# A fused two-layer transformer block: the value products on both halves of the weight columns, in one piece per unit

## Chip, cores and metric

One core of a Trainium2 chip (TensorE = PE for matmuls, VectorE = DVE, ScalarE = ACT, GpSimd = POOL, SyncE = SP, which issues the DMAs). The metric is the device time of one execution in microseconds (us), the median of three runs.

## What is computed

Two transformer layers over x of 1024 tokens by 256 (float32). The change is in the first layer's attention, 16 heads of a latent-attention kind. Cut to what matters:

```python
q = (rmsnorm(h @ q_a_w.T) @ q_b_w.T)          # per head 128 columns without, 64 with rotary embedding
kv = rmsnorm(kv_lora) @ kv_b_w.T              # kv_lora: 1024 keys x 64, shared by the heads
q_pe, k_pe = apply_rope(q_pe, ...), apply_rope(k_pe, ...)
probs = softmax(concat(q_nope, q_pe) @ concat(k_nope, k_pe).T * 192 ** -0.5)
main_out = (probs @ v) @ o_w.T                # v: 128 columns per head
x = x + ga * (gates[0] * main_out + gates[1] * pattern_out)
```

The kernel folds the key and value weights into its query and output weights, so that the keys are 64 latent plus 64 rotary rows per head, and the values are the same 64 latent columns for all heads (`kvx`).

## The kernel before

Engines run lists of steps written by hand (`main_order()` makes the one that matters, MAIN) and meet only by semaphores. MAIN treats 32 **units**: unit u is head pair u // 4 and 256 of the 1024 queries. A unit has four score tiles i = 0 to 3 (head i % 2, 128 queries), each 128 queries by 1024 keys.

For a tile, PE makes the scores (`pe_score`, six matmuls of 512 columns, L1805 to L1807, into one of two double banks; slot i % 2 is free once the exponential two tiles earlier has read it), DVE takes the maximum (`dve_score`, L1814), ACT the exponential with its sum (`act_expo`, L1829), and DVE turns the probabilities in blocks of 32 by 32 (`dve_turn`, L1842) into `PT`: 32 blocks b of 32 keys, each with 128 columns (2 heads x 2 x 32 queries), where the partitions 32g to 32g+31 hold the queries of group g (g = 0 to 3).

The value products of unit u-1 (`pe_pvm`, L1908) are done in **loop** u of `main_order()`, beside the scores of unit u: for each b and g one float32 matmul with 32 rows, 64 weight columns (the values `kv4`) and 128 moving columns, summed over b in PSUM bank 4+g, partitions 0 to 63. The profile shows two records for each float32 matmul, so 256 a unit. Loop u, in the order of the steps:

- step 0: scores (u, 0); projection of unit u-2 (`pe_project_out`, L1935) and its addition to x on DVE (`dve_add_out`, L1948); reciprocals of unit u-1's sums (`dve_recip`, L1862 to L1869); the turn of tile (u-1, 3); exponential (u, 0)
- step 1: scores (u, 1); turn (u, 0); exponential (u, 1)
- step 2: scores (u, 2); value products of u-1, blocks 0 to 15; turn (u, 1); exponential (u, 2)
- step 3: scores (u, 3); blocks 16 to 31; `act_lift` (L1916: the second head's 64 columns from partitions 0 to 63 to 64 to 127); `dve_weigh` (L1926: times the reciprocals `Rs`, into `OTm`); exponential (u, 3); turn (u, 2)

SP sends each unit's reciprocals out (`sp_shares`, L1877, four DMAs after `dve_recip`) and back spread over 64 partitions (`sp_spread`, L1890, two DMAs), in time for `dve_weigh`. The sums, the scores' second bank pair and all other products share PSUM banks 4 to 7, so PE's value products wait for the last `dve_weigh`, and for the copies of all products issued before them (`COPIED`).

Beside this, the tiles of the next head pair p are prepared by six **products** (`PREP_AT` says at which tile numbers, counted from 16(p-1); `FIRST` in what order): four rotary ones R0 to R3 (keys twice, queries twice) and two latent ones Q0, Q1. Each is five or six matmuls of 512 columns on PE (`pe_prep`, L1566); a copy on ACT to the one buffer `t12` (`act_product`, L1600), which waits until the product before has left it; for a rotary product four DMAs on SP that swap rows (`sp_swap`, L1610, after POOL's sum of the rotary product before); and POOL's work (`pool_product`, L1622 to L1648: cosine, sine, sum, rounding, remainder). Scores of a new head pair wait for POOL's parts. Two products that share a loop are called a pair below.

Of the kernel before, what the change touches and what calls it, by code (L numbers as in the profile page):

```python
# [8 lines left out]
F32 = mybir.dt.float32  # L9
# [3 lines left out]
ALU = mybir.AluOpType  # L13
ACT = mybir.ActivationFunctionType
# [57 lines left out]
    (31, 1): [("normed", 0)],  # L72
}

PREP_AT = ((4, 5, 8, 9, 12, 13), (0, 1, 4, 8, 9, 12))


def main_order():

    order = [("expo", 0, 1), ("score", 0, 2), ("ctx", 0), ("ctx", 1), ("vturn", 0, 0), ("expo", 0, 2), ("score", 0, 3),  # L80
             ("cadd", 0), ("ctx", 2), ("vturn", 0, 1), ("cadd", 1), ("expo", 0, 3), ("ctx", 3), ("cadd", 2), ("vturn", 0, 2),
             ("cadd", 3)]
    preps = {16 * (p - 1) + at: (p, i) for p in range(1, 8) for i, at in enumerate(PREP_AT[p > 1])}

    def prep(n):
        if n in preps:
            order.extend([("prep", *preps[n]), ("pcopy", *preps[n])])

    def output(u):
        if u >= 0:  # L90
            order.extend([("project", u), ("add", u)])

    for u in range(1, 32):
        order.append(("score", u, 0))
        output(u - 2)
        prep(4 * u)
        order.extend([("rec", u - 1), ("vturn", u - 1, 3), ("expo", u, 0)])
        order.extend(BESIDE_LAST.get((u, 0), ()))
        order.append(("score", u, 1))
        prep(4 * u + 1)  # L100
        order.extend([("spread", u - 1), ("vturn", u, 0), ("expo", u, 1)])
        order.extend(BESIDE_LAST.get((u, 1), ()))
        order.extend([("score", u, 2), ("pv", u - 1, 0), ("vturn", u, 1), ("expo", u, 2)])
        order.extend([("score", u, 3), ("pv", u - 1, 1), ("lift", u - 1), ("ot", u - 1), ("expo", u, 3), ("vturn", u, 2)])
    output(30)
    order.extend([("rec", 31), ("vturn", 31, 3), ("turn", 0), ("spread", 31), ("pv", 31, 0), ("pv", 31, 1), ("hT", 0),
                  ("wup", 1), ("wdown", 1), ("lift", 31), ("ot", 31), ("project", 31), ("logits", 0), ("add", 31)])
    return order
# [191 lines left out]

R0, R1, R2, R3, Q0, Q1 = ("rope", 0), ("rope", 1), ("rope", 2), ("rope", 3), ("lat", 0), ("lat", 1)

FIRST = (R0, R1, R2, Q0, Q1, R3)


def program(nc, a, out):
    def sem(name):
        return nc.alloc_semaphore(name)
# [6 lines left out]
    def sb(name, shape, dt, at=None):  # L315
        if at is None:
            at = base[0]
            base[0] += size_of(shape, dt)
        return nc.alloc_sbuf_tensor_at(name, list(shape), dt, offset=at)
# [14 lines left out]
    rest = nc.alloc_psum_tensor("bank4", [128, 4, 512], F32)  # L334
# [40 lines left out]
    WSP = A.at  # L375
# [90 lines left out]
    PTl = [sb(f"PTl{i}", [128, 16, 128], F32, at=at) for i, at in enumerate((KV, WKPE))]  # L466
    kv4 = [sb(f"kv4{i}", [128, NT, 64], F32, at=at) for i, at in enumerate((W0A, HN, MP.at, S0 + 88 * 1024))]
    OTm = sb("OTm", [128, 256], F32, at=LNW)
    Rs = sb("Rs", [128, 2, 256], F32, at=vx_end)
    wks = sb("wks", [128, 2, 128], F32, at=vx_end + 2048)  # L470
    wkl = sb("wkl", [128, 2, 128], F32R, at=vx_end + 2048)
# [105 lines left out]
    silu_ok = sem("silu_ok")  # L577
# [1177 lines left out]
    op_tr, op_cT, op_mm, op_add, op_g, op_x = (sem(n) for n in ("op_tr", "op_cT", "op_mm", "op_add", "op_g", "op_x"))  # L1755

    d_kv, pt_ok, lift_ok = sem("d_kv"), sem("pt_ok"), sem("lift_ok")
    d_shares, d_spread = sem("d_shares"), sem("d_spread")
    for s_ in MAIN:
        if s_[0] == "score":  # L1760
# [21 lines left out]
    def transposed(u, b):  # L1782
        return PTl[b // 16][:, b % 16, :] if u == 31 else PT[u % 2][:, b, :]
# [109 lines left out]
    def pe_pvm(e, u, part):  # L1893

        if part == 0:
            if u:
                e.wait_ge(ot_ok[1], u)
                e.wait_ge(add_ok, u)
            else:
                e.wait_ge(op_cT, 4)  # L1900
                e.wait_ge(cadd_ok, 4)
                e.wait_ge(d_kv, 256)
            e.wait_ge(*COPIED[u])
            e.wait_ge(pt_ok, 4 * u + 4)
        for b in range(16 * part, 16 * part + 16):
            for g in range(4):
                rows = slice(32 * g, 32 * g + 32)
                last = e.matmul(rest[0:64, g, 0:128], kv4[b % 4][rows, b // 4, :], transposed(u, b)[rows, :],  # L1908
                                start=(b == 0), stop=(b == 31), skip_group_check=True)
        if part:  # L1910
            last.then_inc(pv_mm[1], 1)

    def act_lift(e, u):

        e.wait_ge(pv_mm[1], u + 1)
        e.activation(rest[64:128, :, 0:64], rest[0:64, :, 64:128], ACT.Copy).then_inc(lift_ok, 1)  # L1916

    def dve_weigh(e, u):

        e.wait_ge(pv_mm[1], u + 1)  # L1920
        e.wait_ge(lift_ok, u + 1)
        e.wait_ge(d_spread, 32 * (u + 1))
        if u:
            e.wait_ge(pr_mm, u)
        by_row = "p (j g q) -> p j g q"
        e.tensor_tensor(OTm[:].rearrange(by_row, j=2, g=4), rest[:, :, 0:64].rearrange("p g (j q) -> p j g q", j=2),  # L1926
                        Rs[:, u % 2, :].rearrange(by_row, j=2, g=4), ALU.mult).then_inc(ot_ok[1], 1)

    def pe_project_out(e, u):

# [1328 lines left out]
```

## Time and profile before

| | |
|---|---|
| runs | 1345.41, 1345.27, 1342.64 us; median 1345.27 |
| profiled execution | 1341.48 us, span of its trace 1339.7 us |
| MAIN's loops | from some 275 us to 805 us of the span |
| busy, share of the span | PE 94%, DVE 65%, ACT 47%, POOL 40% |
| granted PE clock | 0.992 of full speed on average |
| DMA | 66 MB, 49 GB/s on average |

"Busy" of PE counts from a matmul's start to its end; matmuls overlap, so starts tell more than durations. In a timeline row, the first number is the start in us, the second the time covered; the number behind "x" counts the merged instructions. In square brackets stands how long the engine had been idle before it, and what released it.

### The profile page before, as it was taken

Reading aid. Unit: us, or ns where it says so; the run is one execution under the profiler, and the core shown is the slowest. Engines: PE = TensorE matmul, PEld = TensorE weight load, DVE = VectorE, ACT = ScalarE, POOL = GpSimd, SP = SyncE. Lnnn points to the kernel's source line nnn. Section 1 sums busy time; section 2 is a strip of 40 time slices with the busy share of each in tenths; the row PEclk is TensorE's granted clock in tenths of the full one; section 3 lists DMA queues with packets and bytes.
Section 4 is the critical chain, followed back from the end, with each engine's and each line's share of the span. In section 5 each row is a group of like instructions: output and inputs, shape, how many; then the busy total and the mean of one; then the engine's idle time right before and its main releaser. Section 6 shows DMA issues by size and latency. Waiting matters only on the chain. (4 is left out here: it accounts for less than half of the span.)

```text
span 1339.7 us, 34528 instructions
## 1 busy us (share of the span) xinstructions
PE 1260.0 (94%) x14433; PEld 920.9 (69%) x14436; DVE 868.1 (65%) x1322; ACT 634.1 (47%) x1210; POOL 531.6 (40%) x531
## 2 busy tenths in 40 slices
PE   8999999998999999999999998999998998899998
PEld 5544443487777777777777777788864344678997
DVE  4789888165666666666666775645677764565555
ACT  4489888733333333333333333433244766435553
POOL 5266363457757474746574203445200000321221
PEclk9999999999999999999999999999999999899999
DMA  7780010020101010101010204011151510101110
GB/s 283 186 173 2 2 28 7 13 53 24 42 18 43 18 42 18 42 18 39 18 38 18 62 11 139 1 47 48 28 121 41 118 37 1 33 13 36 48 40 32
DMA packets 41700, 66.25 MB, mean 49 GB/s; under 512 B 8477, under 2 KB 27677, under 8 KB 40605
## 3 DMA queue, kind: packets, MB, share of 16 engines
q1 hardware_dynamic: 41544, 64.04, 17.6%
q8 instruction: 115, 1.88, 0.6%
q14 instruction: 41, 0.33, 0.1%
HBM read 45.60 MB, written 8.45 MB: 40 GB/s over the span
## 5 line engine op out<-in xcount | busy, mean ns | idle before, releaser
L1908 PE MATMUL bank<-PT,kv 32*64 32x128 f32 x7936 | 231.2, 269 | 24.1 <-ACT t L1600 23.6
L1908 PEld LDWEIGHTS bank<-PT,kv 32*64 32x64 f32 x7936 | 216.4, 132 | 47.2 <-issue 47.2
L1814 DVE TENSOR_REDUCE nmq<-bank 128x1 f32<-128x1024 f32 x128 | 153.4, 1198 | 88.9 <-PE bank L1807 88.8
L1453 ACT ACTIVATE Pb<-bank 128x512 f32<-128x512 f32 (+3 forms) x355 | 180.6, 573 | 30.1 <-PE bank L1432 9.3
L1303 DVE TENSOR_REDUCE mp<-bank 128x2 f32<-128x1024 f32 x128 | 153.5, 1221 | 27.9 <-PE bank L1295 27.0
L1829 ACT ACTIVATE P<-bank,nmq 128x1024 f32<-128x1024 f32 x128 | 141.8, 1110 | 57.9 <-DVE nmq L1814 57.9
L1842 DVE STREAM_TRANSPOSE PT<-P 128x1024 f32<-128x1024 f32 x124 | 151.8, 1224 | 16.9 <-ACT P L1829 16.8
L1805 PE MATMUL bank<-qk1h,qk0h 128*128 128x512 f32 x256 | 109.9, 429 | 7.8 <-ACT P L1829 7.8
L1374 DVE TENSOR_REDUCE mpc<-bank 128x2 f32<-128x1024 f32 (+2 forms) x96 | 88.3, 953 | 43.2 <-PE bank L1362 22.1
L1475 PE MATMUL bank<-Pb,vx 128*17 128x256 f32 (+3 forms) x1222 | 105.1, 403 | 0.7 <-ACT OTa L1489 0.5
L1807 PE MATMUL bank<-qk1h,qk0l 128*128 128x512 f32 x256 | 101.0, 395 | 0.0
L1806 PE MATMUL bank<-qk1l,qk0h 128*128 128x512 f32 x256 | 100.6, 393 | 0.0
L1916 ACT ACTIVATE bank<-bank 64x256 f32<-64x256 f32 x32 | 11.4, 357 | 187.9 <-PE bank L1908 187.9
L1600 ACT ACTIVATE t<-bank 128x512 f32<-128x512 f32 x48 | 28.7, 598 | 113.4 <-PE bank L1566 68.1
L1622 POOL TENSOR_TENSOR Rt<-t,cosT 128x512 f32<-128x512 f32 x32 | 41.0, 1282 | 104.1 <-ACT t L1600 102.3
L2086 POOL TENSOR_TENSOR cTt<-cTt,gab 128x256 f32<-128x256 f32 x8 | 6.1, 759 | 182.0 <-DVE cTt L2081 181.9
L2312 POOL TENSOR_TENSOR hl<-hf,hh 128x512 fp32r<-128x512 f32 x32 | 41.8, 1306 | 87.1 <-ACT hh L2299 87.1
L1926 DVE TENSOR_TENSOR OTm<-bank,Rs 128x256 f32<-128x256 f32 x32 | 13.6, 424 | 91.2 <-ACT bank L1916 91.2
L1432 PE MATMUL bank<-qstr,kstr 64*128 64x512 f32 x256 | 70.9, 494 | 0.6 <-ACT Pb L1453 0.6
L1805 PEld LDWEIGHTS bank<-qk1h,qk0h 128*128 128x128 f32 x256 | 47.9, 187 | 33.5 <-ACT P L1829 15.1
L2526 POOL TENSOR_TENSOR v1l<-wr,v1h 128x512 fp32r<-128x512 f32 x25 | 32.1, 1286 | 95.3 <-ACT v1h L2521 95.3
L1432 PEld LDWEIGHTS bank<-qstr,kstr 64*128 64x128 f32 x256 | 28.2, 183 | 56.8 <-ACT Pb L1453 36.1
(353 smaller groups left out, 2921.9 us busy)
## 6 DMA issues: line engine op xcount, KB each, us to landing
t<-t SPq DMA_DIRECT2D x128, 64.0 KB, 2.0
wr<-wf SPq DMA_DIRECT2D x25, 256.0 KB, 2.7
wraw<-wf SPq DMA_DIRECT2D x8, 768.0 KB, 4.5
scratch<-stgr SPq DMA_DIRECT2D x4, 1024.0 KB, 4.0
Rs<-shares SPq DMA_DIRECT2D x64, 64.0 KB, 2.7
scratch<-stg SPq DMA_DIRECT2D x8, 384.0 KB, 2.6
qst<-scratch SPq DMA_DIRECT2D x9, 256.0 KB, 8.1
owT<-owT SPq DMA_DIRECT2D x1, 2048.0 KB, 11.4
```

Of the source, the lines that this page charges most:

```text
L1303: e.tensor_reduce(mp[:, w % 3, :, j, kh], wide[slot][:], AX, ALU.max).then_inc(ring_ok, 1)
L1374: e.tensor_reduce(mpc[:, w // 2 % 3, a0:a0 + 2, j, kh], wide[slot][:, :, 0:c], AX, ALU.max).then_inc(ring_ok, 1)
L1432: e.matmul(bank[b][:], kst2[r, hp, kt * 128:kt * 128 + 128], qst2[r, hp, cols(half)], start=True, stop=True).then_inc(st_mm[0], 1)
L1453: e.activation(PBR[l][i % len(PBR[l])][:, 0:c], bank[b][:, 0:c], ACT.Exp, scale=0.25).then_inc(exp_ok[0], 1)
L1475: last = e.matmul(bank[6][32 * a:32 * a + 17, to:to + c], vx[:, t, h * 17:h * 17 + 17], PBR[l][i % len(PBR[l])][:, q0:q0 + c], start=(t == ...
L1805: e.matmul(o, qh[:, qs], kh[:, ks], start=True, stop=False)
L1806: e.matmul(o, qh[:, qs], kl[:, ks], start=False, stop=False)
L1807: last = e.matmul(o, ql[:, qs], kh[:, ks], start=False, stop=True)
L1814: e.tensor_reduce(nmq[:, n % 8:n % 8 + 1], scores(u, i), AX, ALU.max, negate=True).then_inc(mp_ok, 1)
L1829: e.activation(probabilities(u, i)[:], scores(u, i), ACT.Exp, bias=nmq[:, n % 8:n % 8 + 1], accum_out=sums[:, u % 2, i:i + 1]).then_inc(ex ...
L1842: e.transpose(PT[u % 2][:, :, c:c + 32], source).then_inc(pt_ok, 1)
L1908: last = e.matmul(rest[0:64, g, 0:128], kv4[b % 4][rows, b // 4, :], transposed(u, b)[rows, :], start=(b == 0), stop=(b == 31), skip_group ...
```

## The change

- `pe_pvm`: blocks b with even number use weight columns 0 to 63 and write partitions 0 to 63 (columns 64 to 191 of each bank); odd ones use weight columns 64 to 127 and write partitions 64 to 127 (columns 0 to 127). Number and size of the matmuls stay.
- each head's sum now lies in two parts. `act_lift` makes two ACT instructions (64 x 256 each) that bring the half that lies on the wrong partitions to an SBUF buffer `other`; `dve_weigh` adds the two (L1934 of the changed kernel) and then multiplies by `Rs` (L1938), which waits for the spread DMAs only there.
- both halves of a unit's value products stand together before the scores (u, 3): one piece of 256 records.
- `PREP_AT` is one row for all head pairs, (5, 8, 9, 12, 16, 17); `FIRST` has R3 before Q1. ACT's copy of a product stands behind the exponential of its step, and SP takes the list `prep` steps as before.

```diff
-PREP_AT = ((4, 5, 8, 9, 12, 13), (0, 1, 4, 8, 9, 12))
+PREP_AT = (5, 8, 9, 12, 16, 17)
...
-    def prep(n):
+    def prep(n, kind):
         if n in preps:
-            order.extend([("prep", *preps[n]), ("pcopy", *preps[n])])
+            order.append((kind, *preps[n]))
...
         output(u - 2)
-        prep(4 * u)
+        prep(4 * u, "prep")
         order.extend([("rec", u - 1), ("vturn", u - 1, 3), ("expo", u, 0)])
+        prep(4 * u, "pcopy")
         order.extend(BESIDE_LAST.get((u, 0), ()))
         order.append(("score", u, 1))
-        prep(4 * u + 1)
+        prep(4 * u + 1, "prep")
         order.extend([("spread", u - 1), ("vturn", u, 0), ("expo", u, 1)])
+        prep(4 * u + 1, "pcopy")
         order.extend(BESIDE_LAST.get((u, 1), ()))
-        order.extend([("score", u, 2), ("pv", u - 1, 0), ("vturn", u, 1), ("expo", u, 2)])
-        order.extend([("score", u, 3), ("pv", u - 1, 1), ("lift", u - 1), ("ot", u - 1), ("expo", u, 3), ("vturn", u, 2)])
+        order.extend([("score", u, 2), ("pv", u - 1, 0), ("pv", u - 1, 1), ("vturn", u, 1), ("expo", u, 2)])
+        order.extend([("score", u, 3), ("lift", u - 1), ("ot", u - 1), ("expo", u, 3), ("vturn", u, 2)])
...
-FIRST = (R0, R1, R2, Q0, Q1, R3)
+FIRST = (R0, R1, R2, Q0, R3, Q1)
...
-                last = e.matmul(rest[0:64, g, 0:128], kv4[b % 4][rows, b // 4, :], transposed(u, b)[rows, :],
-                                start=(b == 0), stop=(b == 31), skip_group_check=True)
+                c = b % 2
+                last = e.matmul(rest[64 * c:64 * c + 64, g, 64 - 64 * c:192 - 64 * c], kv4[b % 4][rows, b // 4, :],
+                                transposed(u, b)[rows, :], start=(b < 2), stop=(b >= 30), skip_group_check=True)
...
-        e.activation(rest[64:128, :, 0:64], rest[0:64, :, 64:128], ACT.Copy).then_inc(lift_ok, 1)
+        if u:
+            e.wait_ge(sum_ok, SUM0 + u)
+        for hd in range(2):
+            e.activation(other[64 * hd:64 * hd + 64, :, :], rest[64 - 64 * hd:128 - 64 * hd, :, 128 * hd:128 * hd + 64],
+                         ACT.Copy).then_inc(lift_ok, 1)
...
-        by_row = "p (j g q) -> p j g q"
-        e.tensor_tensor(OTm[:].rearrange(by_row, j=2, g=4), rest[:, :, 0:64].rearrange("p g (j q) -> p j g q", j=2),
-                        Rs[:, u % 2, :].rearrange(by_row, j=2, g=4), ALU.mult).then_inc(ot_ok[1], 1)
+        by_row = OTm[:].rearrange("p (j g q) -> p j g q", j=2, g=4)
+        e.tensor_tensor(by_row, rest[:, :, 64:128].rearrange("p g (j q) -> p j g q", j=2),
+                        other[:].rearrange("p g (j q) -> p j g q", j=2), ALU.add).then_inc(sum_ok, 1)
+        e.wait_ge(sum_ok, SUM0 + u + 1)
+        e.wait_ge(d_spread, 32 * (u + 1))
+        e.tensor_tensor(OTm[:], OTm[:], Rs[:, u % 2, :], ALU.mult).then_inc(ot_ok[1], 1)
```

How the order moves, at three places. DVE, from the maximum of tile (u, 3) to the turn of (u, 3), before and after:

```order
L1814 TENSOR_REDUCE nmq<-bank 128x1
L1926 TENSOR_TENSOR OTm<-bank,Rs 128x256
L1842 STREAM_TRANSPOSE PT_159<-P_156 128x32x32
L1814 TENSOR_REDUCE nmq<-bank 128x1
L1948 TENSOR_TENSOR x<-x,bank 128x512
```

```order
L1818 TENSOR_REDUCE nmq<-bank 128x1
L1934 TENSOR_TENSOR OTm<-bank,other 128x256
L1938 TENSOR_TENSOR OTm<-OTm,Rs 128x256
L1846 STREAM_TRANSPOSE PT_159<-P_156 128x32x32
L1818 TENSOR_REDUCE nmq<-bank 128x1
L1959 TENSOR_TENSOR x<-x,bank 128x512
```

The first row's maximum reads scores that PE made between the two pieces before, and makes behind the single piece now; the weighing has become two instructions.

ACT in a loop with a pair of products (`P` are exponentials, `t_152` copies of products), before and after:

```order
L1600 ACTIVATE t_152<-bank 128x512
L1829 ACTIVATE P_156,sums<-bank,nmq 128x1024
L1600 ACTIVATE t_152<-bank 128x512
L1829 ACTIVATE P_157,sums<-bank,nmq 128x1024
L1829 ACTIVATE P_155,sums<-bank,nmq 128x1024
L1916 ACTIVATE bank<-bank 64x4x64
```

```order
L1833 ACTIVATE P_156,sums<-bank,nmq 128x1024
L1603 ACTIVATE t_152<-bank 128x512
L1833 ACTIVATE P_157,sums<-bank,nmq 128x1024
L1603 ACTIVATE t_152<-bank 128x512
L1833 ACTIVATE P_155,sums<-bank,nmq 128x1024
L1924 ACTIVATE other<-bank 64x256 x2
```

Each copy has moved behind the exponential of its step.

SP in the loop of R1 and R2 after the change (`t` are the swaps, `shares` and `Rs` the reciprocals out and back):

```order
L1613 DMA t_152<-t_152 32x512 x4
L1881 DMA shares<-rrow 4x32 x4
L1613 DMA t_152<-t_152 32x512 x4
L1699 DMA wks<-wkpe 128x256
L1894 DMA Rs<-shares 64x2x128 x2
```

Before, the loop with R0 and R1 has the same form (with `wqs` ahead of the shares):

```order
L1610 DMA t_152<-t_152 32x512 x4
L1702 DMA wqs<-wqpe 128x256
L1877 DMA shares<-rrow 4x32 x4
L1610 DMA t_152<-t_152 32x512 x4
L1890 DMA Rs<-shares 64x2x128 x2
```

The second swap and the weights' load stand ahead of the spread in both pairs; what has moved is when the second copy lets that swap go.

## Rows read from the trace of the kernel before

**Rows 1.** The page, part 1: busy time of each engine.

```profile
PE 1260.0 (94%) x14433; PEld 920.9 (69%) x14436; DVE 868.1 (65%) x1322; ACT 634.1 (47%) x1210; POOL 531.6 (40%) x531
```

**Rows 2.** Windows: a pair, a pair, one product, none; length, busy (count), clock, DMA share.

```profile
533.22:551.63 18.41, 16.99 (x297) 14.36 (x296) 10.93 (x13) 5.95 (x11) 10.68 (x12) 1.00 0.15 38
...
567.55:585.93 18.38, 16.61 (x295) 14.08 (x294) 10.70 (x13) 5.95 (x11) 11.50 (x13) 1.00 0.06 18
585.93:601.86 15.93, 15.54 (x291) 12.94 (x290) 10.60 (x13) 5.58 (x10) 4.96 (x5) 1.00 0.09 23
768.99:784.03 15.04, 14.40 (x286) 11.99 (x285) 10.61 (x14) 5.19 (x11) 0.00 (x0) 1.00 0.04 10
```

**Rows 3.** Timeline of PE in loop 29, which has no product.

```profile
772.64 0.50 PE L1805 MATMUL bank<-qk1h,qk0h 128*128 128x512 f32 x1
...
777.20 0.50 PE L1805 MATMUL bank<-qk1h,qk0h 128*128 128x512 f32 x1 [0.64 <-ACT P L1829]
...
778.79 3.72 PE L1908 MATMUL bank<-PT,kv 32*64 32x128 f32 x128
782.45 0.50 PE L1805 MATMUL bank<-qk1h,qk0h 128*128 128x512 f32 x1
...
784.03 3.72 PE L1908 MATMUL bank<-PT,kv 32*64 32x128 f32 x128
```

**Rows 4.** Timeline of PE and weight loads with four column tiles, and of both kinds counted.

```profile
204.82 0.63 PE L1475 MATMUL bank<-Pb,vx 128*17 128x256 f32 x8
...
204.80:205.00 0.20, 0.18 (x4) 0.13 (x8) 1.00 0.00 0
...
285.43:285.55 0.12, 0.10 (x4) 0.12 (x8) 1.00 0.00 0
```

**Rows 5.** Timeline of DVE in the same loop 29.

```profile
773.22 0.42 DVE L1926 TENSOR_TENSOR OTm<-bank,Rs 128x256 f32<-128x256 f32 x1 [2.90 <-ACT bank L1916]
773.56 1.23 DVE L1842 STREAM_TRANSPOSE PT<-P 128x1024 f32<-128x1024 f32 x1
774.72 1.19 DVE L1814 TENSOR_REDUCE nmq<-bank 128x1 f32<-128x1024 f32 x1
775.83 0.67 DVE L1948 TENSOR_TENSOR x<-x,bank 128x512 f32<-128x512 f32 x1
...
776.95 1.20 DVE L1842 STREAM_TRANSPOSE PT<-P 128x1024 f32<-128x1024 f32 x1
...
784.14 1.23 DVE L1814 TENSOR_REDUCE nmq<-bank 128x1 f32<-128x1024 f32 x1 [1.47 <-PE bank L1807]
```

**Rows 6.** Timeline of ACT: exponential of loop 29; two copies of a pair.

```profile
775.94 1.12 ACT L1829 ACTIVATE P<-bank,nmq 128x1024 f32<-128x1024 f32 x1 [1.70 <-DVE nmq L1814]
...
609.49 0.60 ACT L1600 ACTIVATE t<-bank 128x512 f32<-128x512 f32 x1 [2.37 <-PE bank L1566]
...
614.11 0.60 ACT L1600 ACTIVATE t<-bank 128x512 f32<-128x512 f32 x1 [2.93 <-DMA t<-t]
```

**Rows 7.** Timeline of PE: value products behind the pair's second copy.

```profile
614.96 3.72 PE L1908 MATMUL bank<-PT,kv 32*64 32x128 f32 x128 [1.34 <-ACT t L1600]
```

**Rows 8.** Timeline of SP's issues, and DMAs by line (last number: us to landing).

```profile
610.12 2.49 SPq L1610 DMA_DIRECT2D t<-t  x4
...
562.13 0.58 SPq L1696 DMA_DIRECT2D wks<-wkpe  x1
...
599.70 1.35 SPq L1890 DMA_DIRECT2D Rs<-shares  x2
...
Rs<-shares SPq DMA_DIRECT2D x64, 64.0 KB, 2.7
```

**Rows 9.** Timeline of POOL: rounding, behind the sum, of the product copied at 609.49.

```profile
616.82 1.28 POOL L1641 CAST qk1h<-Rt 64x512 fp32r<-64x512 f32 x2
```

**Rows 10.** Timeline of PE: value products of the last unit and its projection.

```profile
808.09 7.76 PE L1908 MATMUL bank<-PTl,kv 32*64 32x128 f32 x256 [1.71 <-DVE PTl L1845]
816.81 1.13 PE L1935 MATMUL bank<-mo,OTm 128*128 128x256 f32 x4 [0.96 <-DVE OTm L1926]
```

More of the change, by code:

```diff
@@ L82, in main_order @@
              ("cadd", 3)]
-    preps = {16 * (p - 1) + at: (p, i) for p in range(1, 8) for i, at in enumerate(PREP_AT[p > 1])}
-    def prep(n):
+    preps = {16 * (p - 1) + at: (p, i) for p in range(1, 8) for i, at in enumerate(PREP_AT)}
+    def prep(n, kind):
         if n in preps:
-            order.extend([("prep", *preps[n]), ("pcopy", *preps[n])])
+            order.append((kind, *preps[n]))
     def output(u):
@@ L468, in program @@
     OTm = sb("OTm", [128, 256], F32, at=LNW)
+    other = sb("other", [128, 4, 64], F32, at=WSP + 6144)
     Rs = sb("Rs", [128, 2, 256], F32, at=vx_end)
@@ L1757, in program @@
     d_kv, pt_ok, lift_ok = sem("d_kv"), sem("pt_ok"), sem("lift_ok")
+    sum_ok, SUM0 = silu_ok, 2
     d_shares, d_spread = sem("d_shares"), sem("d_spread")
@@ L1915, in act_lift @@
         e.wait_ge(pv_mm[1], u + 1)
-        e.activation(rest[64:128, :, 0:64], rest[0:64, :, 64:128], ACT.Copy).then_inc(lift_ok, 1)
+        if u:
[3 more added lines that the diff above has]
+                         ACT.Copy).then_inc(lift_ok, 1)
     def dve_weigh(e, u):
         e.wait_ge(pv_mm[1], u + 1)
-        e.wait_ge(lift_ok, u + 1)
-        e.wait_ge(d_spread, 32 * (u + 1))
+        e.wait_ge(lift_ok, 2 * u + 2)
         if u:
             e.wait_ge(pr_mm, u)
-        by_row = "p (j g q) -> p j g q"
-        e.tensor_tensor(OTm[:].rearrange(by_row, j=2, g=4), rest[:, :, 0:64].rearrange("p g (j q) -> p j g q", j=2),
-                        Rs[:, u % 2, :].rearrange(by_row, j=2, g=4), ALU.mult).then_inc(ot_ok[1], 1)
+        by_row = OTm[:].rearrange("p (j g q) -> p j g q", j=2, g=4)
[4 more added lines that the diff above has]
+        e.tensor_tensor(OTm[:], OTm[:], Rs[:, u % 2, :], ALU.mult).then_inc(ot_ok[1], 1)
     def pe_project_out(e, u):
```

## The prediction

> **What bounds the kernel now.** I read the page's busy times first. PE stands at 94% of the span, DVE at 65% [rows 1]. Then the windows of single loops: a loop with a pair of products takes 18.4 us, with one 15.93, with none 15.04, and PE is busy for 14.4 of those 15.04 us, DVE for 10.6 [rows 2]. Loops 2 to 30 are 14 of the first kind, 12 of the second and 3 of the third: 14 x 18.4 + 12 x 15.93 + 3 x 15.04 = 493.9 us. The PE timeline of a loop without product shows where it goes: two pieces of value products take 3.66 and 3.65 us from their start to the next score [rows 3], nearly half the loop. One PE wait is left, 0.64 us before the scores of step 2, for the exponential that frees their bank [rows 3]. In a pair PE waits 1.34 us for the second copy [rows 7]. So PE bounds MAIN, but the chains behind DVE and ACT are close.
>
> **The value products.** Each half piece is 128 records in 3.65 us: four a wave, one for each group of 32 rows, 0.114 us a wave. A wave uses 64 of the 128 weight columns. Do two column halves run beside each other? The trace has a near relative: L1475 has four matmuls with 17 weight columns on four column places. In the first 0.20 us all four first records have started, and all eight records (256 columns, float32) are covered by 0.63 us [rows 4]; one after the other, eight records of twice the columns of a value product could not be done in that time, as each alone would need about a wave of the value products times two, 0.22 us, 1.8 us in all. So column places do overlap, with different moving data. Ends of the range: full overlap, 32 waves of eight, 3.65 us for the 256 records; none, about 7.14 us. I take 3.65, since rows 4 show overlap by four and this asks for two. What could spoil it is the load of weights, eight of 64 columns per 0.114 us; a stretch of eight loads takes 0.12 to 0.13 us in both kinds [rows 4].
>
> A rule speaks against the change. The same rows show eight weight loads in the first 0.12 us of a piece beside only four matmuls, so four loads went to row groups whose matmuls were running [rows 4]. The Trainium skill, TensorE: Matmul & The Clock Gate, Part 3, "The mechanism", says that a weight load overlaps running matmuls only when the row group differs. By that rule nothing would be won from the second column half, and the time would be that of the third rival below; this trace disagrees with it already.
>
> The join of the pieces saves a switch from full array to row groups and back: 784.03 - 782.45 = 1.58 us for six score matmuls against 1.38 at 0.23 each, and a little at the return, some 0.3 us of PE a loop. It needs no term of its own, because PE stops being the bound.
>
> **What bounds a loop then.** PE would need 15.04 - 3.5 - 0.3 - 0.64 = 10.6 us, DVE 10.6 + 0.45 (one more instruction). So I follow the chain. Count from S, the first score matmul of step 3 (now right behind the value products), by intervals of the rows:
> - maximum (u, 3) starts at 1.69 (782.45 to 784.14, DVE idle before it) [rows 3, 5];
> - the sum follows at 2.80 (a maximum holds DVE 1.11 us), the multiplication at 3.25 (0.42 us and the wait for itself, by the weighing of before), the turn at 3.59 [rows 5]. Today ACT's move and its wait are over at 0.58, where the weighing starts, so a second move of 64 x 256 ends by 1.2 at the latest: hidden by that maximum;
> - maximum (u+1, 0) at 4.75, its exponential 1.22 us later at 5.97, scores of step 2 another 1.26 later at 7.23, value products 1.59 later at 8.82 [rows 3, 5, 6];
> - next S 3.65 later: **12.47 us** for a loop with no product. Before, the weighing came at 0.58 instead of 3.25 because the maximum (u, 3) stood ahead of the second piece; this is the new wait that eats part of the gain. Behind the multiplication PE's projection also waits, some 0.9 us, hidden by the same chain.
>
> **The products** [rows 5 to 9]. Maximum 4.75 + 1.11 + 1.12 = 6.98 for the turn of (u, 3), 8.10 for maximum (u+1, 1), its exponential at 9.32. Copies stand behind the exponentials now, 1.09 us after their start (an exponential's 1.12 less the small overlap):
> - one product at step 0 (Q0): copy at 7.06, done before PE needs it. 12.47.
> - one at step 1 (R0): copy at 10.41; value products 0.85 behind (614.11 to 614.96), 11.26; next S **14.91**.
> - pair R1, R2 or R3, Q1: first copy at 7.06, the second 4.7 behind (4.62 in rows 6, which name the DMA; I add a little for a fuller SP queue), because the swap's DMAs must have read the buffer: 11.76; value products 12.61; next S **16.26**.
> - In the loop of R1, R2 the second swap waits for POOL's sum of R1, 7.33 us behind the copy (609.49 to 616.82), so 14.4. Then 2.49 us of issues, 0.58 for weights, the first spread 0.65: the second spread leaves at 18.15 and lands 2.7 us later, 20.85, which is 4.59 in the next loop. Its multiplication was due at 3.25, so the loop of Q0 takes 12.47 + 1.35 = **13.82**.
>
> Each four loops thus take 14.91 + 16.26 + 13.82 + 16.26 = 61.25 against 68.7. DVE's work, 4 x 11.05 = 44 us, fits, and so does POOL's, 5 to 11.5 us in a loop with products [rows 2].
>
> **The sum.** Loops 2 to 30 now hold 7 + 7 pairs, 6 of R0, 7 of Q0, 2 with none (the last copy has moved to loop 28): 14 x 16.26 + 6 x 14.91 + 7 x 13.82 + 2 x 12.47 = 438.8, against 493.9: -55.1. The first unit's products in loop 1: two pieces and six scores, 8.89 us [rows 3], become 3.65: -5.2. In loop 31, DVE has the next layer's statistics as well and sets the end (its turn releases the last piece [rows 10]); it starts its sum 2.2 us later than its weighing before and has 0.45 more: +2.65. The last unit's 256 records, 7.76 us, lose half: -3.75, and the second move and the multiplication show there, +0.75 [rows 10]. Total -60.7. On the profiled execution's 1341.5 us that gives 1280.8. The median of the runs is 3.8 above that execution, so I forecast **1285 us** for the median. The order of R3 and Q1 in the stage before MAIN, and the extra move on ACT, cost nothing: ACT is busy for 5.2 to 6 us of a loop [rows 2], and the scores that start MAIN need neither of the two.
>
> **Rivals.**
> - Weight loads bound the waves of eight: 0.13 instead of 0.114 us, or a wave starts late behind the other half's. For it: loads come at twice the density that any row shows. Some 0.6 to 0.9 us a unit, 20 to 28 in all less the 5 us of late spread that this hides: **1303**.
> - The side chains are longer than counted: POOL does R1, R2 and Q0 in a row, each some 10 us by the sum's 7.33 us and the rounding behind it [rows 9], and the next head pair's first scores wait for all three; by my walk they are ready some 1.6 us early, and the spread lands 0.6 us or more early in the other loops. If each of 21 loops loses 0.9 us: **1303** as well, with another face (PE waits before step 0, DVE waits for the DMA).
> - No overlap of the column halves (also what would follow if the change did not do what it says): all waits of the new order stay and nothing is won. 3.5 us x 31 + 3.75 = 112, less the 9.5 us of late spread that would be hidden: -60.7 + 102.5 = +42, **1387**, slower. It decides as soon as the 256 records take over 5.5 us instead of 3.65 (60.7 / 32 = 1.9 more). Against it stand rows 4.
> - The swaps land sooner or the second copy costs less than 4.7 us, since SP is less crowded when the copy leaves later: pairs at 15 instead of 16.26, 14 x 1.3 = 18 less: **1267**.
>
> **The numbers.** Forecast 0.55; weight loads 0.14; longer side chains 0.14; faster pairs 0.10; no overlap 0.05; something that lies within 0.2% (about what a measurement of this kernel can tell from no change) 0.02. The range goes from 1263, just below the faster pairs, to 1318, which takes in each 1303 case and most of both together (1321); it leaves out the slower case and the tails. Faster by over 0.2%: 0.93, same 0.02, slower 0.05.
>
> **What would show it.** In the changed profile the value products' rows must read x256 with some 3.9 us covered, where two rows of 3.72 stood; 7.2 or more would be no overlap, 4.3 to 4.8 the weight loads. DVE's maximum (u, 3) must start 1.7 us behind the first score matmul, the sum directly behind it, and a loop without product must take 12.5 us. In loops of pairs PE must wait some 2 us for ACT's copy, in loops of R0 some 2 us too, and in loops of Q0 the multiplication must wait over a microsecond for the spread's DMA. PE's share must fall well below 94% and no engine be near it. If pairs take 18 us still, the copies' chain was worth more than I gave it; if the loop without product is longer than 13 us at 3.65 us of value products, my chain through DVE misses a wait.

## The result, and the profile after

The changed kernel takes **1379.8 us** (median of four runs, 1366.5 to 1381.3) against 1344.9 for the kernel before: ratio 1.023, 95% interval [1.020, 1.027]. It is slower; 1285 was forecast, and the range (1263 to 1318) does not hold it. The profiled execution took 1381.25 us, its trace 1379.4. All times compare executions in the same, undisturbed state; one execution of a later kernel ("Sum in PSUM") took 2482.3 us at full clock and is left out.

Page of the changed kernel, part 1 and the chain that ended last, answering to [rows 1]:

```profile
PE 1197.7 (87%) x14433; PEld 852.0 (62%) x14436; DVE 888.5 (64%) x1354; ACT 651.8 (47%) x1242; POOL 534.2 (39%) x531
...
PE 57%; DVE 17%; issue 11%; DMA 5%; SPq 4%; ACT 4%; POOL 1%; ACTq 0%; DVEq 0%; POOLq 0%
```

PE is no longer near full, as forecast, and yet the time rose. The word to see is "issue", 11% of the chain: time in which PE waited for nothing that the profile shows.

Windows of loops from one first score matmul of step 3 to the next (pair, pair, one product at step 1, none; columns as in [rows 2]), and last a piece of another loop:

```profile
514.05:532.24 18.19, 13.83 (x300) 10.87 (x295) 11.06 (x14) 6.56 (x12) 14.32 (x15) 1.00 0.15 38
698.53:716.72 18.19, 13.31 (x297) 10.70 (x295) 10.94 (x14) 6.56 (x12) 7.34 (x7) 1.00 0.10 24
716.72:734.39 17.67, 12.47 (x296) 10.01 (x291) 11.80 (x14) 6.07 (x11) 7.04 (x9) 1.00 0.11 27
804.64:819.11 14.47, 11.34 (x289) 8.79 (x284) 11.11 (x15) 5.85 (x12) 0.00 (x0) 1.00 0.05 12
508.46:511.80 3.34, 3.34 (x140) 3.34 (x147) 1.43 (x2) 1.21 (x2) 1.16 (x1) 0.57 0.34 81
```

Forecast were 16.26, 16.26, 14.91 and 12.47. All four ran at full clock (1.00), with one gap of 1.6 to 1.8 us in the value products of each; over loops 2 to 31 the means were 19.5 (14 pairs), 17.7 (6 of R0), 16.6 (7 of Q0) and 15.0 (3 of none).

PE's timeline in the loop without product at 804.64, answering to [rows 3]:

```profile
804.64 0.50 PE L1809 MATMUL bank<-qk1h,qk0h 128*128 128x512 f32 x1
...
811.92 0.51 PE L1809 MATMUL bank<-qk1h,qk0h 128*128 128x512 f32 x1 [0.97 <-ACT P L1833]
...
813.50 3.10 PE L1913 MATMUL bank<-PT,kv 32*64 32x128 f32 x198
818.04 1.15 PE L1913 MATMUL bank<-PT,kv 32*64 32x128 f32 x58 [1.43 <-issue]
819.11 0.50 PE L1809 MATMUL bank<-qk1h,qk0h 128*128 128x512 f32 x1
```

And DVE's, answering to [rows 5]:

```profile
806.35 1.23 DVE L1818 TENSOR_REDUCE nmq<-bank 128x1 f32<-128x1024 f32 x1 [1.53 <-PE bank L1811]
807.49 0.41 DVE L1934 TENSOR_TENSOR OTm<-bank,other 128x256 f32<-128x256 f32 x1
807.94 0.43 DVE L1938 TENSOR_TENSOR OTm<-OTm,Rs 128x256 f32<-128x256 f32 x1
808.28 1.24 DVE L1846 STREAM_TRANSPOSE PT<-P 128x1024 f32<-128x1024 f32 x1
809.44 1.19 DVE L1818 TENSOR_REDUCE nmq<-bank 128x1 f32<-128x1024 f32 x1
```

The chain is as forecast almost to the digit: maximum at 1.71 (1.69), sum 2.85 (2.80), multiplication 3.30 (3.25), turn 3.64 (3.59), next maximum 4.80 (4.75), scores of step 2 at 7.28 (7.23), value products 8.86 (8.82). Then the records run at the forecast rate, 128 in some 1.83 us where before took 3.45: the column halves overlap in full. But after 198 of them PE stands still, with no engine to wait for, and the piece takes 5.61 us to the next score instead of 3.65.

Two more pieces, from PE's timeline of the changed kernel:

```profile
600.03 2.23 PE L1913 MATMUL bank<-PT,kv 32*64 32x128 f32 x137 [1.61 <-ACT t L1603]
603.50 2.01 PE L1913 MATMUL bank<-PT,kv 32*64 32x128 f32 x119 [1.24 <-issue]
...
617.15 1.78 PE L1913 MATMUL bank<-PT,kv 32*64 32x128 f32 x102
619.85 2.08 PE L1913 MATMUL bank<-PT,kv 32*64 32x128 f32 x128 [0.91 <-issue]
623.86 0.67 PE L1913 MATMUL bank<-PT,kv 32*64 32x128 f32 x26 [1.92 <-issue]
```

Between the last two halts lie 128 matmuls and 128 weight loads, 256 instructions. The window between the halts before counts two of the same (254 + 254, and four semaphore instructions make 512):

```profile
603.50:619.85 16.35, 13.29 (x254) 10.50 (x254) 12.14 (x14) 5.40 (x10) 14.49 (x15) 0.90 0.13 33
```

PE's own instructions come by DMA. The page of the changed kernel counts them in a queue of their own, and 115 packets of 16384 bytes for 14433 + 14436 matmuls and loads and 603 other instructions of PE is one packet for 256:

```profile
q8 instruction: 115, 1.88, 0.6%
```

Number PE's instructions from the start of the trace: every one of the 27 gaps over 0.5 us inside a piece (from the start of one matmul to the start of the next) stands at number 193 modulo 256. Call the passing of such a number a boundary. The packets' starts in the trace give the price of a block. In MAIN the next packet leaves 0.7 to 1.4 us after a boundary in 41 of 71 cases, and no boundary was passed sooner than 2.2 us after the last packet's start; in the gaps it was 2.3 to 2.9. So a block takes PE **some 3 to 4.3 us at least** (the two nearest boundaries are 2.9 us apart), and 256 instructions of the new pieces want 1.83. Before, 256 instructions of the value products were 3.45 us of work, 5 with the scores between pieces: just enough. In its 530 us of MAIN the kernel before had one such gap, of 0.74 us, at number 193 too.

A second kind of gap is hidden among the 27. In 21 of them the boundary before lay 2.9 to 4.3 us back: the block was used up too fast. In the other 6 it lay 6.7 to 15.1 us back, and its packet left only 4 to 12 us behind it, in five of the six 0.5 to 1.2 us into the piece. There the gap comes from a late packet (a **late gap** below); what holds it back is not shown.

The Trainium skill, Runtime: NRT & Kernel Launch, section "Instruction fetch mechanics", has blocks of 16 KiB, 256 instructions, which this trace confirms (115 packets for 29472 instructions). It also calls the cost of a crossing "mostly hidden" and gives PE room for 2048 instructions, four times a unit's 512. The gaps of 0.7 to 2.5 us within those 512 disagree.

### The profile page after: what moved, and what is told of

It reads as the page before. It is cut to its first block, busy times and chain, and to the rows that moved or that the text cites. A ratio compares the mean times of both kernels' runs of the same rounds, so it can differ in the third digit from the quotient of the medians.

```text
span 1379.4 us, 34624 instructions
## 1 busy us (share of the span) xinstructions
PE 1197.7 (87%) x14433; PEld 852.0 (62%) x14436; DVE 888.5 (64%) x1354; ACT 651.8 (47%) x1242; POOL 534.2 (39%) x531
## 3 DMA queue, kind: packets, MB, share of 16 engines
q8 instruction: 115, 1.88, 0.6%
## 4 chain that ended last, share of the span: by engine, by line
PE 57%; DVE 17%; issue 11%; DMA 5%; SPq 4%; ACT 4%; POOL 1%; ACTq 0%; DVEq 0%; POOLq 0%
PE bank L1913 8%; PE bank L1478 7%; PE bank L2122 5%; PE bank L2123 5%; PE bank L2124 5%; PE bank L1435 4%; SPq L1613 3%; DVE nmq L1818 3%; DVE PT L1846 3%; PE bank L1298 2%; DMA t<-t 2%; PE bank L1809 2%; DVE mpc L1377 2%; PE bank L1415 2%; DMA Rs<-shares 2%
## 5 line engine op out<-in xcount | busy, mean ns | idle before, releaser
L1913 PE MATMUL bank<-PT,kv 32*64 32x128 f32 x7936 | 151.8, 303 | 88.3 <-ACT t L1603 47.1
L1913 PEld LDWEIGHTS bank<-PT,kv 32*64 32x64 f32 x7936 | 137.6, 148 | 107.8 <-issue 107.6
L1924 ACT ACTIVATE other<-bank 64x256 f32<-64x256 f32 x64 | 24.3, 380 | 127.4 <-PE bank L1913 126.5
L1946 PE MATMUL bank<-mo,OTm 128*128 128x256 f32 x128 | 39.4, 434 | 42.1 <-DVE OTm L1938 42.0
L1627 POOL TENSOR_TENSOR t<-t,sinT 128x512 f32<-128x512 f32 x32 | 40.8, 1274 | 71.6 <-DMA t<-t 71.6
```

The lines of the kernel that those rows point to most:

```text
L1913: last = e.matmul(rest[64 * c:64 * c + 64, g, 64 - 64 * c:192 - 64 * c], kv4[b % 4][rows, b // 4, :], transposed(u, b)[rows, :], start=(b ...
```

## Where the forecast's time went

For each of the 30 loops from the second on, the trace gives how far each interval lies above the forecast:

| interval | us above forecast, 30 loops |
|---|---|
| gaps inside the pieces | 45.5 |
| rest of the piece (half clock; 0.28 a loop also in quiet ones) | 26.7 |
| multiplications over 0.42 us | 13.1 |
| sum late: scores of step 3 at half clock (3.0), or two gaps between them (3.6) | 6.6 |
| rest up to the value products | 6.8 |
| late spreads of Q0 loops, in the forecast, mostly absent | -9.5 |
| sum | 89.2 |

For the profiled execution the whole is 1381.25 - 1280.8 = 100.4 us; the other 11.2 lie in loop 1 (3.4) and behind the first score of step 3 in loop 31 (7.8). The two gaps between scores, at 550.42 and 791.14, are of 1.17 and 2.77 us from start to start and stand at number 193 too: the scores miss blocks like the value products, and only the 27 inside pieces are counted above. A piece took 6.06 us on average to the next score: 3.65 forecast + (45.5 + 26.7) / 30.

Two items are new here. **Clock:** 21 stretches of MAIN, 78.5 us, have a granted clock of half speed (1.2 GHz), where the kernel before has none. Twelve begin about the end of a PE wait of 2.0 to 3.1 us for a copy, as below; five stand at waits of 1.8 to 4.4 us for DVE, and four behind gaps of missing instructions, 1.9 to 2.4 us idle:

```profile
508.46 5.66 PE L1913 MATMUL bank<-PT,kv 32*64 32x128 f32 x256 [2.25 <-ACT t L1603]
```

This piece had 0.57 in its first 3.34 us (last row of the windows) and shows no gap, and it lasts as long as one with gaps. **Multiplication:** in 14 of 32 units it takes 0.8 to 1.5 us beside a POOL instruction instead of 0.42. The changed kernel's DVE and POOL:

```profile
720.00 1.29 DVE L1938 TENSOR_TENSOR OTm<-OTm,Rs 128x256 f32<-128x256 f32 x1
...
718.39 2.62 POOL L1651 TENSOR_TENSOR qk0l<-t,qk0h 64x512 fp32r<-64x512 f32 x2
```

It began while POOL's instruction ran and ended just behind it (721.3 against 721.0). Before, the weighing read one operand from PSUM and took 0.42 us in all 32.

## Experiments

Each was timed beside the kernel before; ratios are to it. "Numbered gaps" are gaps over 0.5 us inside pieces, all 32 units.

**Order alone, columns alone.** The first takes the kernel before and gives it the change's `main_order`, `PREP_AT` and `FIRST`; the second takes the changed kernel and gives it those of before.

> The kernel before with the change's order alone: the 256 records of a unit in one piece ahead of the last scores, copies behind exponentials, R3 ahead of Q1; one half of the weight columns, the old move and weighing. Theory A (instruction supply: PE's instructions come in blocks of 256, and the next block is usable some 3.5 to 4.0 us after the block ahead of it was begun): 128 records on one column half last 3.45 us, so a block is used up about when the next is there; inside a piece at most a few gaps of 0.1 to 0.5 us, a piece 7.3 to 7.9 us, time 1375 to 1400 us. Theory B (a long piece stops after half of it by itself, whatever the instructions): a gap of 1.2 us or more in the middle of most pieces, some 8.8 us a piece, 1415 us or more.

> The kernel before with the two column halves alone: its own order, a unit's records in two pieces of 128 with the scores of step 3 between them, its own places for the copies. Theory A (instruction supply in blocks of 256, 3.5 to 4.0 us each): the two pieces begin 1.83 + 1.4 = 3.2 us apart or more, so a block boundary in each costs 0.2 to 0.8 us, and not the 1.2 to 2.5 us of the changed kernel; all gaps inside pieces lie at one and the same instruction number modulo 256; 1270 to 1320 us. Theory B (a long piece stops by itself): no gap at all in pieces of 128 records, 1.83 us each, 1250 to 1290 us. Theory C (the column halves themselves make PE halt, as each second half is switched in): gaps of 1.2 us or more in most pieces of 128, 1340 us or more.

Order alone: 1395.8 us, 1.0387 [1.0352, 1.0422]. Columns alone: 1315.0 us, **0.9802 [0.9762, 0.9842]**. Timelines of PE, order alone and then columns alone:

```profile
515.21 7.27 PE L1910 MATMUL bank<-PT,kv 32*64 32x128 f32 x256 [2.21 <-ACT t L1602]
534.50 8.72 PE L1910 MATMUL bank<-PT,kv 32*64 32x128 f32 x256 [2.38 <-ACT t L1602]
```

```profile
563.10 2.05 PE L1911 MATMUL bank<-PT,kv 32*64 32x128 f32 x125 [1.76 <-ACT t L1601]
566.54 0.43 PE L1911 MATMUL bank<-PT,kv 32*64 32x128 f32 x3 [1.39 <-issue]
...
595.77 2.10 PE L1911 MATMUL bank<-PT,kv 32*64 32x128 f32 x128 [1.35 <-ACT t L1601]
599.39 2.10 PE L1911 MATMUL bank<-PT,kv 32*64 32x128 f32 x128
```

A long piece at 3.45 us for 256 instructions has next to no gap (3 numbered ones, 2.0 us): theory B falls. Its 8.72 us is half clock again, 44 us of MAIN. In columns alone the two pieces begin 3.6 us apart (595.77 and 599.39), and most boundaries cost nothing. Eleven gaps are left, 18.0 us; my 0.2 to 0.8 in every piece was the wrong shape. Only three of the eleven have the boundary before within 4 us. In the other eight it lies 5.5 to 15 us back and the packet left late: for the gap shown it was passed at 560.7, in the scores ahead of PE's wait, and the packet left at 564.2, 1.1 us into the piece. So the two edits pull apart: the column halves give 27 to 30 us in the old order, the new order costs 51 alone, and together they cost 35.

**Few columns**, from the kernel before, leaving out half of the queries in the value products:

```diff
-last = e.matmul(rest[0:64, g, 0:128], kv4[b % 4][rows, b // 4, :], transposed(u, b)[rows, :],
+last = e.matmul(rest[0:64, g, 0:64], kv4[b % 4][rows, b // 4, :], transposed(u, b)[rows, 0:64],
```

> The kernel before, in which the value products leave out the queries 64 to 127 (64 moving columns instead of 128); the number of instructions, the order and the single column half are those of before. Theory A (instruction supply): the same 256 instructions a piece now need about 1.8 us of PE, so gaps at block boundaries appear although no column half was added, 0.2 to 0.8 us each; time as the kernel with the column halves alone, within 15 us. Theory C (the column halves make PE halt): pieces of 1.8 us with no gap, 1250 to 1290 us, well below the kernel with the column halves alone. If the records keep their 0.114 us a wave of four, a record has a floor that is not its columns, and the time stays at 1345.

1299.1 us, 0.9658 [0.9621, 0.9695]. Timeline of PE:

```profile
552.39 2.08 PE L1908 MATMUL bank<-PT,kv 32*64 32x64 f32 x125 [1.81 <-ACT t L1600]
556.10 0.33 PE L1908 MATMUL bank<-PT,kv 32*64 32x64 f32 x3 [1.63 <-issue]
```

Twelve numbered gaps, 18.5 us, with one column half and the old instructions, so theory C falls: pieces of 256 instructions in 1.9 us meet the gaps, with one column half as with two. The time is 16 us below columns alone, just outside the 15 expected.

**Apart.** The changed kernel with `("pv", u - 1, 1)` moved back behind `("score", u, 3)`.

> The changed kernel with the two halves of a unit's records apart again: 128 ahead of the scores of step 3, 128 behind them, and the rest as changed. Theory A (instruction supply): a gap of 0.2 to 0.8 us at a block boundary instead of 1.2 to 2.5, and in the pause between pieces the next block comes; against the changed kernel 1.0 to 1.5 us a loop less, 1330 to 1350 us. Theory B (a long piece stops by itself): no gap, 1310 to 1325 us. Theory C (column halves): gaps as long as in the changed kernel, 1375 us or more.

1345.3 us, 1.0007 [0.9974, 1.0040]. Nine numbered gaps, 15.8 us, instead of 27 with 46.5; half clock in 15 stretches still. Join or split of the piece is worth 35 us. Six of the nine gaps that stay are late ones, against 6 of 27: it is the gaps of blocks used up too fast that the split took away (3 left of 21).

**Spaced.** The changed kernel with work that delays the second boundary:

```diff
             e.wait_ge(pt_ok, 4 * u + 4)
+        elif u < 31:
+            qh, _, kh, _ = tiles_of(2 * ((u + 1) // 4))
+            for _ in range(16):
+                e.matmul(bank[4][:, 256:512], qh[:, 0:128], kh[:, 0:256], start=True, stop=True, skip_group_check=True)
```

> The changed kernel with 16 useless matmuls of 256 columns (some 1.84 us of PE in 32 instructions, into columns of a bank that nobody reads) in the middle of the piece, between records 128 and 129, for every unit but the last. Supply theory (the next block of 256 instructions is usable 3.5 to 4.0 us after the one ahead of it was begun): the two boundaries that a unit's records cross are now at least 1.83 + 1.84 = 3.7 us apart, so the gaps of 1.2 to 2.5 us vanish (under 10 us in all inside the halves, where the changed kernel has 47.6), and the time stays within 8 us of 1380 although PE does 31 x 1.84 = 57 us more. Rival (the gaps are no matter of the time between boundaries; PE halts a second or two in each long piece whatever is in it): gaps stay and the work comes on top, 1420 us or more.

1403.6 us, 1.0439 [1.0401, 1.0477]. Timeline of PE:

```profile
820.29 2.10 PE L1917 MATMUL bank<-PT,kv 32*64 32x128 f32 x128
822.32 2.17 PE L1912 MATMUL bank<-qk1h,qk0h 128*128 128x256 f32 x16
824.41 2.09 PE L1917 MATMUL bank<-PT,kv 32*64 32x128 f32 x128
```

The gaps went, from 46.5 us to 10.8 (7 of them, at 193), though the records are the same: it is the time between boundaries, and five of the seven that stay are late ones, which room between boundaries doesn't mend. The total missed my 8 us: it rose by 24. The added work took some 2.1 us a unit (822.32 to 824.41), 65 us in all, of which 41 were free; it runs at half clock too where the piece does, up to 3.7 us instead of 2.1.

**Filler.** 12 such matmuls ahead of `wait_ge(*COPIED[u])`, in the loops with a copy at step 1.

> The changed kernel, in which PE does 12 useless matmuls of 256 columns (some 1.4 us, into columns that nobody reads) ahead of its wait for the second copy, in the 20 loops with a copy at step 1; their result goes nowhere, and the rest is computed as before. Clock theory (the half clock in 20 or so stretches follows PE's waits of 2 us and more for the copies): the wait is filled, most of the half-clock stretches go, the pieces run at full clock and then meet the missing block instead; time 1365 to 1378 us, since a piece at half clock lasted hardly longer than one with gaps. If the half clock cost what its 68 us suggest (34 us), 1345 us. If PE's waits don't bring it about, stretches and time stay.

1365.0 us, 1.0160 [1.0112, 1.0208]. Timeline of PE, one wait:

```profile
549.53 1.59 PE L1910 MATMUL bank<-qk1h,qk0h 128*128 128x256 f32 x12
552.13 3.12 PE L1917 MATMUL bank<-PT,kv 32*64 32x128 f32 x201 [1.01 <-ACT t L1603]
556.66 1.13 PE L1917 MATMUL bank<-PT,kv 32*64 32x128 f32 x55 [1.42 <-issue]
```

Half clock from 68 to 20 us between loops 2 and 31, "rest of the piece" from 26.7 to 9.4, and gaps instead: 33 numbered, 51.7 us, none of them late. The clock theory holds for the stretches behind the waits for copies. The net gain of some 15 us is less sure: the two intervals touch, and not all of it need be the clock's, as the long multiplications fell too, from 13.1 to 7.0 us, and the late spreads rose from 1.5 to 6.1.

**Sum in PSUM**, from the changed kernel:

```diff
-e.tensor_tensor(by_row, rest[:, :, 64:128]..., other[:]..., ALU.add).then_inc(sum_ok, 1)
+both = rest[:, :, 64:128]
+e.tensor_tensor(both, both, other[:], ALU.add).then_inc(sum_ok, 1)
...
-e.tensor_tensor(OTm[:], OTm[:], Rs[:, u % 2, :], ALU.mult).then_inc(ot_ok[1], 1)
+e.tensor_tensor(OTm[:]..., both..., Rs[:, u % 2, :]..., ALU.mult).then_inc(ot_ok[1], 1)
```

> The changed kernel with the sum of the two halves written back into PSUM, so that the multiplication by the shares reads PSUM and SBUF as before the change. Theory P (the multiplication of 1.3 to 1.5 us in 14 of 32 loops comes from both its inputs being in SBUF while POOL works there): it takes 0.42 us in all 32 loops, and a good part of 14 x 1 us is won, 1365 to 1375 us. Rival (the operation is stretched by something else, a late DMA or the clock): a dozen of multiplications still take over 0.7 us, 1380 us.

1365.2 us (median of three), 1.0143 [1.0071, 1.0214]. One line of the source view, for the changed kernel and for this one:

```profile
L1938 DVE TENSOR_TENSOR OTm<-OTm,Rs x32: 424/464/1524, 295.7 to 852.3; 128x256 f32<-128x256 f32 x32
```

```profile
L1938 DVE TENSOR_TENSOR OTm<-bank,Rs x32: 424/424/425, 292.7 to 826.8; 128x256 f32<-128x256 f32 x32
```

Theory P holds: the long multiplications are gone, and their 13.1 us in the table fall to 0.1. The time fell by 15 us, but the two intervals touch, so the traces show this gain better than the times do. The Trainium skill, SBUF — State Buffer, section "SBUF: two separate sides", has this rule: a DVE operation with two SBUF inputs and a GpSimd operation that reads SBUF exclude each other; the one that starts first holds the other back. The traces agree: 14 of 32 multiplications over 0.6 us with two inputs in SBUF, none with one in PSUM.

**Half of the blocks.** The changed kernel with `range(16 * part, 16 * part + 8)` in `pe_pvm` and the stops at b >= 22.

> The changed kernel with half of the key blocks left out of the value products: 128 records, 256 instructions, in one piece. Theory A (supply): no second boundary can be met before the next block has come, so at most one or two gaps over 0.25 us inside pieces; 1.83 us a piece. Undisturbed loops then show the forecast chain less 1.82 us: 10.7 without product, 13.1 with R0, 14.4 with a pair. The sum for the whole would be 1280.8 - 31 x 1.82 = 1224 us; what the run takes more is the price of the half clock and of the long multiplications, which this kernel keeps: 1230 to 1260 us. Theory B (a long piece stops by itself) expects no gap either, but says nothing of where the gaps of the other kernels lie.

1304.1 us, 0.9707 [0.9682, 0.9732], not 1230 to 1260. Gaps are few (5 numbered, 8.8 us), but late spreads cost 29.4 us, which the forecast had in Q0 loops alone: once loops are short, SP's queue and the shares' DMAs set their pace. With 17 half-clock stretches this suggests that **my sum would not have been reached with all instructions in time either**.

**Five on the way to a better kernel**, all from columns alone. The first adds the sum in PSUM; the second also writes step 3 as

```diff
-("pv", u - 1, 1), ("lift", u - 1), ("ot", u - 1), ("expo", u, 3), ("vturn", u, 2)
+("pv", u - 1, 1), ("expo", u, 3), ("vturn", u, 2), ("lift", u - 1), ("ot", u - 1)
```

The third and the fourth start from that: `("pcopy", ...)` of a loop's only product behind `("expo", u, 0)`; `("rec", u)` behind `("vturn", u, 2)` instead of a loop later. The fifth has both.

> The kernel before with the two column halves, its own order, and the sum written back into PSUM. Theory P: against the column halves alone some 0.5 us in each of half the loops, 1300 to 1310 us. Rival: 1315 us. Gaps inside pieces stay at instruction number 193 modulo 256, in 10 to 20 pieces.

> As the kernel with column halves, its own order and the sum in PSUM, but behind the scores of step 3 the exponential and the turn of step 2's block come ahead of the move and the weighing (ACT and DVE stood idle there for 2.7 and 1.7 us, waiting for the second piece). Chain theory: maximum (u+1, 0) comes 0.8 to 1.1 us sooner in each of 30 loops, 1275 to 1285 us. Supply theory on top: pieces move closer, so that more of them meet a block that is not there, and PE waits more often at half clock; then 1285 to 1300. If the second copy of pairs set the loop by itself, the gain would be had in the other half of the loops only.

> The turned kernel, with the copy of a loop's only product behind the exponential (as the change has it), and the first copy of a pair ahead of it as before. Chain theory: in 12 loops the exponential (u+1, 0) comes 1.7 us sooner (it waits for the copy at 8.33 us, though its maximum is done at 7.0) and with it the scores of step 2 and the value products: 12 x 1.4 = 17 us less, 1288 us. Supply theory: part of it is lost again at missing blocks, 1288 to 1300.

> The turned kernel, with reciprocal and shares of a unit ahead of the weighing of the one before, where DVE stood idle for a microsecond, instead of behind maximum (u+1, 0). The spread leaves some 4 us sooner: no multiplication waits for it any more (in the turned kernel it does in ten loops, 0.5 to 1.6 us), and DVE has 0.5 us less in its chain between two maxima. Chain theory: 0.5 us in 30 loops, at most, and 8 us for the late spreads: 1283 to 1295 us. Rival: the shares' DMAs now stand ahead of the first swap on SP's queue, and the second copy of a pair comes later by it; 1305 or more.

> Both of the last two edits together: the sum of their gains if they are apart, 1270 to 1282 us; if missing instruction blocks now set the pace of the value products, their gains don't add up, and it stands at 1285 or more with 20 or more gaps inside pieces.

| kernel | us | ratio | numbered gaps, us |
|---|---|---|---|
| columns and PSUM | 1304.7 | 0.9715 [0.9673, 0.9756] | 11, 18.0 |
| turned | 1304.9 | 0.9711 [0.9660, 0.9763] | 11, 13.1 |
| singles | 1304.1 | 0.9708 [0.9677, 0.9739] | 9, 12.2 |
| reciprocal early | 1312.2 | 0.9764 [0.9737, 0.9792] | 12, 19.1 |
| both | 1300.2 | 0.9683 [0.9640, 0.9726] | 7, 15.5 |

Theory P again gives its 10 us. The other four missed what I expected: "turned" has its maximum 0.7 us sooner in quiet loops (5.86 against 6.55 behind the score of step 3) and no time to show for it. In pairs the second copy sets the loop, 4.8 us behind the first, and the turn ahead of the weighing makes the first later: the weighing ends 0.42 us later, PE's projection and the product behind it wait for that, the first copy comes at 8.33 us instead of 7.9 and a quiet pair takes 16.0 us instead of 15.6. In the other loops of "both" a gain is there (13.0 us for one product at step 0, 13.5 in columns alone), but it lies within the spread of gaps and clock. "Reciprocal early" met the number of its rival, 1305 or more. Of these five only that one and "both" have intervals that don't overlap (0.9737 against 0.9726); no other order among them is shown, only that each beats both kernels. Windows of "both", one product and a pair:

```profile
676.40:689.38 12.98, 12.25 (x293) 9.68 (x290) 10.13 (x14) 4.97 (x9) 3.03 (x3) 1.00 0.10 23
660.39:676.40 16.01, 13.65 (x296) 10.79 (x295) 12.55 (x15) 7.44 (x14) 12.11 (x13) 1.00 0.08 21
```

Over the 15 traces there are 187 numbered gaps, and all stand at 193 modulo 256, though the kernels execute from 21280 to 30467 instructions of PE.

## Why the prediction was wrong

- *"Full overlap, 32 waves of eight, 3.65 us for the 256 records."* The overlap was right (128 records in 1.83 us). The term failed at the step from rate to piece: I asked whether the array and its weight loads keep up, not whether the instructions do. Measured: 6.06 us a piece, of which 1.5 are gaps for instructions and 0.9 the rest, half clock above all. The trace had the figure that should have warned me: 256 instructions of PE in 3.45 us was the densest stretch of the old kernel, and I doubled that density with no row that shows it. The overlap I read from eight records [rows 4], far too few to reach the end of a block.
- *The rival without overlap "decides as soon as the 256 records take over 5.5 us".* That point was right: at 6.06 the change loses. Its own price, 1387, met order alone at 1395.8. Only its mechanism was wrong, and with it the 0.05.
- *The chain through DVE and ACT, 8.82, 11.26 and 12.61 us to the value products:* right to 0.1 us in quiet loops; 26.5 us over 30 loops were lost in the others, 13.1 of them in the multiplication. *"0.42 us"* for it was read from an operation with one operand in PSUM.
- *"PE stops being the bound", so its pauses cost nothing:* they cost the clock in part. Order alone has 13 stretches at half clock in MAIN with the old rate of records; its pieces take 7.15 us to the next score at full clock and 8.8 at half clock.
- *The late spread, 1.35 in Q0 loops:* 0.2 measured, since the loops were longer; real in the shorter loops of half the blocks, and larger than I had it (2.5 us in Q0 loops, and 0.8 on average in those of pairs, where I had none).
- *The joined piece "saves a switch ... some 0.3 us":* joining was the harmful half of the change. The scores between the pieces were what gave the next block most of its time. Apart against changed: 35 us.
- *Loop 1, -5.2, and the last unit, -3.75:* the first score of step 3 in loop 1 came 3.4 us later than before, where the forecast had it in the same place (289.1); the last piece took 5.6 us instead of 7.76, a gap of 1.27 in it.

## What to carry to other kernels

Count instructions of PE for each stretch, not only columns: matmuls with few columns, each with a weight load, can outrun the supply, and the profile shows it as "issue", always at the same instruction number modulo 256. Spread such bursts between long matmuls rather than joining them, above all when an edit makes each cheaper. A wait of PE ahead of a burst is no help by itself, since the packet may leave late. And when an edit takes the bound off PE, read the granted clock behind its new waits, and keep one operand of a DVE product in PSUM where POOL is at work.

## What the runs showed of the chip that I had not expected

- A block of 256 instructions costs PE some 3 to 4.3 us when it is used up faster; the packet itself takes 1.1 us. All 187 numbered gaps end 2.2 to 3.0 us behind the start of the last packet.
- In 78 of the 187 the boundary before lay over 4.8 us back, and its packet left only 2.3 to 13 us behind it, in 60 of the 78 between 0.3 and 1.8 us into the piece. In 57 PE had waited for another engine in between; with those waits filled (filler) none of 33 gaps is of this kind. But a wait is not the whole of it: behind the boundary at 607.6 the packet left at 617.0, when PE had been back at work since 610.6. What triggers it stays open. Nor is a packet always that of the very next block: in the kernel before six boundaries were passed 0.3 to 2.1 us behind a packet's start, with no gap over 0.5 us.
- Two halves of 64 weight columns with the same rows run fully beside each other: 128 records of 128 columns in 1.83 us, 3.45 in one half.
- A record of 64 columns takes little more than half of one of 128 (1.88 us for 128 records in few columns, 3.45 with 128 columns).
- Half clock and missing blocks hide each other: a piece at half clock lasts 5.7 us without a gap, one with gaps 5.0 to 8.6.
